# Gate stage of a GNN and mixture-of-experts kernel: one Gelu instead of two, its parts made on VectorE, transposed activations evicted by ScalarE, logits two steps later

## The chip, the cores and the metric

One core of one Trainium2 chip runs the whole program. The metric is the device time of one execution in microseconds. The kernel before was timed three times, and the number given is the median.

## What is computed

The reference, cut to what matters here (the graph layer ahead of it gives `x`, 12500 nodes of 256 features, in float32):

```python
# C = 256, HID = 1024, E = 8, 12500 rows; xf is the layer norm of x
H = gelu(xf @ W1 + b1)                       # 12500 x 1024, exact gelu
probs = softmax(H @ Wg + bg)                 # 12500 x 8
assign = argmax(probs)
out = 0
for e in range(8):
    y = H @ Wd[e] + bd[e]
    out += where(assign == e, probs[:, e] * y, 0)
x = x + out
```

The change touches only the stage that makes `H`, the eight logits of each row and the row's place in the list of its expert.

## The kernel before

The program runs in stages, one after the other: it sorts the edges, sends and collects the messages, runs the two linear layers of the graph part, then the **gate** stage, then the **experts** stage. Each stage is a block in which every engine has its own written-out order of instructions. Semaphores alone tie the engines together; there is no planner.

**The gate stage** (function `gate`, from L1419) walks over 25 chunks of 512 rows (`CN`; chunk number `i`, buffer slot `s` = `i` modulo 2). Each chunk has 8 steps `k` (`KC`), one for each 128 of the 1024 hidden columns. In step `k`:

- TensorE makes `ps_h` (128 hidden columns x 512 rows) from six products of 512 columns (L1857): the inputs are split into a high and a low part in a rounded float format, `w_hi`, `w_lo`, `xnT_hi`, `xnT_lo`. Below this is h(k).
- ScalarE applies Gelu to it twice, once into `act_h` in float32 (L1629) and once into `act_hi`, the rounded high part (L1630). Below, gelu(k).
- VectorE subtracts the two into `act_lo` (L1696, `keep_rest`).
- TensorE turns `act_h` back to rows with four transposes into `ps_b` (L1808, `back`), and adds two products to the logits `ps_g` (L1817 and L1818, `add_logits`). Both are done for step `k - 1` after h(k).
- VectorE copies `ps_b` into the payload `pay` of the chunk (L1705, `keep_back`), for step `k - 1` ahead of `keep_rest(k)`.

`act_h`, `act_hi`, `act_lo`, `ps_h`, `ps_b` and `pay` have two buffers each; `ps_g`, `ps_x`, `gT` and the places have one.

Spread over these steps, at fixed step numbers, is the work of the neighbouring chunks. For the chunk that follows: step 0 turns the graph layer's output (`turn_back` L1790, made ready by ScalarE in `second_output` L1606) and adds the residual (`residual` L1666); step 2 takes the moments of the rows (`moments`, L1671 to L1674 and a chain of small linked instructions); step 4 normalises (L1682); step 5 turns the result (`turn_xn` L1799), and ScalarE (L1612) and VectorE (L1689, `keep_xnT_rest`) split it into high and low. For the chunk that went before: step 0 copies the summed logits (`keep_logits` L1620), step 1 turns them (`turn_logits` L1831) and VectorE chooses the expert (`choose`, L1711 to L1724), step 3 counts (`count`, L1841 and L1844) and finds the places (`find_places`, L1729 to L1740).

When the places of a chunk are known (`where_ready`), GpSimd's queue issues four indirect DMAs (`send`, L1575), which write the chunk's payload of 512 rows x 5168 bytes to the regions of the experts in DRAM, and then copies the next residual into the payload (L1589). A slot of `pay` can be written again only when its four transfers have landed: step 0's eviction of chunk `i` waits for the transfers of chunk `i - 2` (`sent[s]`), which share its slot. That eviction is issued in step 1. With the names of the code, in the chunk's step `k == 1`:

```python
def keep_back(i, s, k, before):
    if k == 0 and later(i, 2):
        dve.wait_ge(sent[s], 16 * CH * before)
```

TensorE's first product to `ps_g` of a chunk (`add_logits(i, 0)`) waits until `keep_logits(i - 1)` has emptied it (`logit_kept`). Instructions that depend on one another on VectorE are tied by `steps.link`, which waits until the first has ended.

Of the kernel before, what the change touches and what calls it, by code (L numbers as in the profile page):

```python
# [11 lines left out]
ACT = mybir.ActivationFunctionType  # L12
AX = mybir.AxisListType

P = 128
# [5 lines left out]
KC = HID // P  # L21
# [3 lines left out]
CH = 4  # L25
# [3 lines left out]
LAST = NCH - 1  # L29
# [45 lines left out]
TTILES = N // P + NE  # L75

RESIDUAL_AT = 0
TURN_LOGITS_AT = 1
CHOOSE_AT = 1
MOMENTS_AT = 2  # L80
COUNT_AT = 3
PLACE_AT = 3
NORMALISE_AT = 4
XN_AT = 5

# [1333 lines left out]
def gate(nc, c, x, w1, b1, wg, bg, wd, hid, expert_w, scale, shift, regions, ends):  # L1419
# [5 lines left out]
    with ExitStack() as ctx:  # L1425
# [8 lines left out]
        act_hi = m.sb("act_hi", [P, 2, CN], F32R)  # L1434
        act_lo = m.sb("act_lo", [P, 2, CN], F32R)
        fold = m.sb("fold", [2 * NE, NE])
        b_sb = m.sb("b_sb", [P, KC])
# [7 lines left out]
        act_h = m.sb("act_h", [P, 2, CN])  # L1445
        pay = m.sb("pay", [P, 2, CH, PAY])
# [25 lines left out]
        ps_h = m.ps("ps_h", [P, 2, CN])  # L1472
        ps_b = m.ps("ps_b", [P, 2, CH, P])
# [37 lines left out]
        def all_chunks(eng, chunk):  # L1511

            chunk(0, 0, 0)
            chunk(1, 1, 0)
            with eng.Fori(1, LAST // 2, 1) as i:
                chunk(2 * i, 0, i)
                chunk(2 * i + 1, 1, i)
            chunk(LAST, 0, LAST // 2)

        def later(i, by=1):  # L1520
            return not isinstance(i, int) or i >= by
# [4 lines left out]
        with nc.Block() as block:  # L1526
# [35 lines left out]
            @block.gpsimd  # L1562
            def _(pool):


                pool.iota(token_i[:], [[P, CH]], base=0, channel_multiplier=1).then_inc(iotas, 1)  # L1566
                pool.iota(first_i[:], [[CAP, PAIRS_E], [CAP - 1, 2]], base=0, channel_multiplier=0).then_inc(iotas, 1)
                pool.iota(sign_i[:], [[0, PAIRS_E], [-2, 2]], base=1, channel_multiplier=0).then_inc(iotas, 1)

                def send(i, s):  # L1570
                    pool.wait_ge(where_ready, i + 1)
                    pool.wait_ge(x2_copied, i + 1)
                    pool.sem_inc(pool_turn, 1)
                    for j in range(CH):
                        pool.indirect_dma_start(  # L1575
                            out=regions[:, :],
                            out_offset=bass.IndirectOffsetOnAxis(ap=where_i[:, s, j:j + 1], axis=0),
                            in_=pay[:, s, j, :], in_offset=None,
                        ).then_inc(sent[s], 16)

                def chunk(i, s, before):
                    if later(i):
                        send(i - 1, 1 - s)

                    if later(i, 2):
                        pool.wait_ge(sent[s], 16 * CH * before)
                    pool.wait_ge(residual_ready, i + 1)
                    pool.sem_inc(pool_turn, 1)
                    pool.tensor_copy(pay[:, s, :, PAY_X:PAY_X + D], x2[:, s]).then_inc(x2_copied, 1)  # L1589

                all_chunks(pool, chunk)
                send(LAST, 0)
                for s in range(2):
                    pool.wait_ge(sent[s], 16 * CH * (LAST // 2 + 1 - s))

            @block.scalar
            def _(act):
                act.wait_ge(params_in, 16 * PARAMS)

                def second_output(i):  # L1600

                    if later(i):
                        act.wait_ge(turned_back, i)
                        act.sem_inc(act_turn, 1)
                    for k in range(DH):
                        ins = act.activation(out2[:, k, :], hid[:, ds(i, 1), k, :].rearrange("p o n -> p (o n)"), ACT.Relu,  # L1606
                                             scale=scale[:, k:k + 1], bias=shift[:, k:k + 1])
                    ins.then_inc(out2_ready, 1)

                def keep_xnT(i, s):  # L1610
                    act.wait_ge(xn_turned, i + 1)
                    act.activation(xnT_hi[:, s], ps_x[:].rearrange("p c f -> p (c f)").rearrange("p (k n) -> p k n", k=DH),  # L1612
                                   ACT.Copy).then_inc(xnT_hi_ready, 1)

                def keep_logits(i):
                    act.wait_ge(logit_sum, i + 1)
                    if later(i):
                        act.wait_ge(logit_done, i)
                        act.sem_inc(act_turn, 1)
                    act.activation(gT[:], ps_g[0:2 * NE, :], ACT.Copy).then_inc(logit_kept, 1)  # L1620

                def chunk(i, s, before):
                    if not is_last(i):
                        second_output(i + 1)
                    for k in range(KC):
                        act.wait_ge(h_done, KC * i + k + 1)

                        act.sem_inc(act_turn, 1)
                        act.activation(act_h[:, k % 2, :], ps_h[:, k % 2, :], ACT.Gelu, bias=b_sb[:, k:k + 1])  # L1629
                        act.activation(act_hi[:, k % 2, :], ps_h[:, k % 2, :], ACT.Gelu, bias=b_sb[:, k:k + 1]).then_inc(h_ready, 1)  # L1630
                        if k == 0 and later(i):
                            keep_logits(i - 1)
                        if k == XN_AT and not is_last(i):
                            keep_xnT(i + 1, 1 - s)

                second_output(0)
                keep_xnT(0, 0)
                all_chunks(act, chunk)
                keep_logits(LAST)

            @block.vector
            def _(dve):
# [49 lines left out]
                def keep_rest(i, k):  # L1692

                    dve.wait_ge(h_ready, KC * i + k + 1)
                    dve.sem_inc(dve_turn, 1)
                    dve.tensor_tensor(act_lo[:, k % 2, :], act_h[:, k % 2, :], act_hi[:, k % 2, :].bitcast(F32),  # L1696
                                      ALU.subtract).then_inc(act_lo_ready, 1)

                def keep_back(i, s, k, before):

                    if k == 0 and later(i, 2):

                        dve.wait_ge(sent[s], 16 * CH * before)
                    dve.wait_ge(back_done, KC * i + k + 1)
                    dve.tensor_copy(pay[:, s, :, k * P:(k + 1) * P], ps_b[:, k % 2, :, :]).then_inc(back_ready, 1)  # L1705

                def choose(i, s):

# [33 lines left out]
                def chunk(i, s, before):  # L1742
                    steps.restart()
                    for k in range(KC):
                        if k > 0:
                            keep_back(i, s, k - 1, before)
                        elif later(i):
                            keep_back(i - 1, 1 - s, KC - 1, None)
                        keep_rest(i, k)
                        if not is_last(i):  # L1750
                            if k == RESIDUAL_AT:
                                residual(i + 1, 1 - s)
                            if k == MOMENTS_AT:
                                moments(i + 1, 1 - s)
                            if k == NORMALISE_AT:
                                normalise(i + 1, 1 - s)
                            if k == XN_AT:
                                keep_xnT_rest(i + 1, 1 - s)
                        if later(i):
                            if k == CHOOSE_AT:  # L1760
                                choose(i - 1, 1 - s)
                            if k == PLACE_AT:
                                find_places(i - 1, 1 - s)
# [5 lines left out]
                keep_xnT_rest(0, 0)  # L1769
                all_chunks(dve, chunk)  # L1770
                steps.restart()
                keep_back(LAST, 0, KC - 1, None)
                choose(LAST, 0)
                find_places(LAST, 0)

# [4 lines left out]
            def _(pe):  # L1780
# [66 lines left out]
                def chunk(i, s, before):  # L1847
                    for k in range(KC):
# [4 lines left out]
                            pe.wait_ge(h_ready, KC * i + k - 1)  # L1853

                        for q in range(DH):
                            for w, a in ((w_hi, xnT_hi), (w_hi, xnT_lo), (w_lo, xnT_hi)):
                                ins = pe.matmul(ps_h[:, k % 2, :], w[:, q, k * P:(k + 1) * P], a[:, s, q, :],  # L1857
                                                start=(q == 0 and w is w_hi and a is xnT_hi),
                                                stop=(q == DH - 1 and w is w_lo))
# [8 lines left out]
                            count(i - 1)  # L1868
                        if k == XN_AT and not is_last(i):
                            turn_xn(i + 1)  # L1870
                        if k > 0:
                            add_logits(i, k - 1)
                        elif later(i):
                            add_logits(i - 1, KC - 1)
                        if k == 0 and not is_last(i):
                            turn_back(i + 1)

# [1 line left out]
                turn_xn(0)  # L1879
                all_chunks(pe, chunk)  # L1880
                back(LAST, KC - 1)
                add_logits(LAST, KC - 1)
                turn_logits(LAST)
                count(LAST)

# [310 lines left out]
```

## Time and profile before

| | us |
|---|---|
| median of 3 runs (lowest, highest) | 3603.17 (3600.44, 3605.65) |
| the profiled execution, its own time | 3586.81 |
| its span, first to last instruction | 3585.0 |
| gate stage, first VectorE instruction to the last | 2459.5 to 3120.6 |
| busy: TensorE, VectorE, ScalarE, GpSimd | 2979.3, 2553.1, 1208.6, 781.5 |

The profile is of one execution. Busy time of TensorE includes the drain of pipelined matmuls, so neighbouring matmuls overlap: a product of 512 columns is shown with 0.39 us and the next one starts 0.23 us after it. In the same way an instruction of ScalarE or VectorE that does not depend on the one ahead of it starts about 0.1 us before that one's shown end. Distances between starts are therefore the safer measure, and the sections below use them.

### The profile page before, as it was taken

Reading aid. Unit: us, or ns where it says so; the run is one execution under the profiler, and the core shown is the slowest. Engines: PE = TensorE matmul, PEld = TensorE weight load, DVE = VectorE, ACT = ScalarE, POOL = GpSimd, SP = SyncE. Lnnn points to the kernel's source line nnn. Section 1 sums busy time; section 2 is a strip of 40 time slices with the busy share of each in tenths; the row PEclk is TensorE's granted clock in tenths of the full one; section 3 lists DMA queues with packets and bytes.
Section 4 is the critical chain, followed back from the end, with each engine's and each line's share of the span. In section 5 each row is a group of like instructions: output and inputs, shape, how many; then the busy total and the mean of one; then the engine's idle time right before and its main releaser. Section 6 shows DMA issues by size and latency. Waiting matters only on the chain. (4 is left out here: it accounts for less than half of the span.)

```text
span 3585.0 us, 67096 instructions
## 1 busy us (share of the span) xinstructions
PE 2979.3 (83%) x20000; PEld 2445.8 (68%) x20001; DVE 2553.1 (71%) x6181; ACT 1208.6 (34%) x2051; POOL 781.5 (22%) x731
## 2 busy tenths in 40 slices
PE   2666667888888886999999999896898889659998
PEld 1233336777777776888888888444676767559998
DVE  5999977777777775777777777335778787676665
ACT  2221103655656653000000000264454545353332
POOL 1211103555555553000000000000122222212222
PEclk9777887999999998999999999998999999879999
DMA  2323105878888887999999999001233334266664
GB/s 75 140 89 105 56 1 195 312 298 308 311 310 308 318 310 278 329 331 329 332 330 330 334 328 332 7 0 32 111 148 135 147 135 160 119 221 210 211 210 146
DMA packets 214716, 751.08 MB, mean 210 GB/s; under 512 B 28411, under 2 KB 64549, under 8 KB 189430
## 3 DMA queue, kind: packets, MB, share of 16 engines
q1 hardware_dynamic: 130694, 446.18, 36.8%
q0 software_dynamic: 83952, 304.02, 21.7%
q8 instruction: 37, 0.61, 0.1%
q14 instruction: 33, 0.27, 0.0%
HBM read 411.44 MB, written 353.16 MB: 213 GB/s over the span
## 5 line engine op out<-in xcount | busy, mean ns | idle before, releaser
L1214 PE MATMUL coll_ps_sum<-coll_rows,coll_hot 128*128 128x256 f32 x3724 | 823.9, 381 | 18.4 <-DVE coll_hot L1155 18.3
L1214 PEld LDWEIGHTS coll_ps_sum<-coll_rows,coll_hot 128*128 128x128 f32 x3724 | 702.3, 191 | 111.1 <-DVE coll_hot L1155 20.3
L1155 DVE TENSOR_SCALAR coll_hot<-coll_nodes,coll_rows 128x128 f32<-128x128 f32 x1862 | 494.7, 342 | 228.0 <-PE coll_ps_sum L1214 165.6
L915 PE MATMUL send_ps_msg<-send_window,send_pick 128*128 128x256 f32 x3584 | 537.7, 299 | 23.6 <-ACT send_msg L948 17.4
L948 ACT ACTIVATE send_msg<-send_ps_msg 128x1024 f32<-128x1024 f32 x448 | 456.4, 1026 | 279.2 <-PE send_ps_msg L915 196.9
L796 POOL DMA_INDIRECT messages<-send_msg,send_to x448 | 469.7, 1048 | 369.6 <-ACT send_msg L948 213.1
L915 PEld LDWEIGHTS send_ps_msg<-send_window,send_pick 128*128 128x128 f32 x3584 | 472.2, 199 | 29.8 <-ACT send_msg L948 19.1
L839 DVE TENSOR_SCALAR send_pick<-send_ps_local,edges_down 128x1024 fp32r<-128x1024 f32 x224 | 287.6, 1284 | 199.7 <-PE send_ps_local L902 143.4
L1247 ACT ACTIVATE nodes_hid<-coll_ps_turned 128x256 f32 (+1 forms) x98 | 37.5, 383 | 811.2 <-PE coll_ps_turned L1059 811.2
L2130 PE MATMUL exp_ps_y<-exp_w_hi,exp_hT_hi 128*128 x840 | 246.5, 293 | 1.0 <-DVE exp_hT_lo L2082 1.0
L2130 PE MATMUL exp_ps_y<-exp_w_hi,exp_hT_lo 128*128 x840 | 238.1, 283 | 0.0
L2130 PE MATMUL exp_ps_y<-exp_w_lo,exp_hT_hi 128*128 x840 | 237.9, 283 | 0.0
L1629 ACT ACTIVATE gate_act_h<-gate_ps_h,gate_b_sb 128x512 f32<-128x512 f32 x200 | 137.3, 686 | 290.1 <-PE gate_ps_h L1857 289.1
L1566 POOL IOTA gate_token_i<- 128x4 int32 x1 | 0.1, 131 | 1044.1 <-POOLq L1292 1044.1
L1575 POOL DMA_INDIRECT regions<-gate_pay,gate_where_i x100 | 109.9, 1099 | 522.0 <-DVEq L1740 499.2
L538 DVE TENSOR_REDUCE sort_place<-sort_banks 128x8 f32<-128x784 f32 x224 | 186.0, 866 | 20.5 <-PE sort_banks L664 18.5
L2026 ACT ACTIVATE exp_hT_hi<-exp_ps_t 128x1024 fp32r<-128x1024 f32 x105 | 107.7, 1026 | 263.7 <-PE exp_ps_t L2119 263.7
L660 PE MATMUL sort_banks<-sort_offset,edges_spread 128*128 128x396 f16 x448 | 121.5, 358 | 68.0 <-DVE sort_place L538 53.3
L1696 DVE TENSOR_TENSOR gate_act_lo<-gate_act_h,gate_act_hi 128x512 fp32r<-128x512 f32 x200 | 139.4, 697 | 51.0 <-ACT gate_act_hi L1630 50.4
L2002 POOL DMA_INDIRECT out_dram<-exp_res,exp_token x105 | 103.2, 983 | 332.5 <-DVE exp_res L2101 330.6
L2082 DVE TENSOR_TENSOR exp_hT_lo<-exp_ps_t,exp_hT_hi 128x1024 fp32r<-128x1024 f32 x105 | 128.6, 1225 | 60.1 <-ACT exp_hT_hi L2026 60.1
L1705 DVE COPY gate_pay<-gate_ps_b 128x512 f32<-128x512 f32 x200 | 138.0, 690 | 45.2 <-PE gate_ps_b L1808 35.0
(300 smaller groups left out, 5177.0 us busy)
## 6 DMA issues: line engine op xcount, KB each, us to landing
coll_rows<-messages SPq DMA_DIRECT2D x98, 1300.0 KB, 7.5
coll_rows<-messages SPq DMA_DIRECT2D x98, 1170.0 KB, 7.4
exp_pay<-regions SPq DMA_DIRECT2D x105, 646.0 KB
send_window<-node_table SPq DMA_DIRECT2D x112, 256.0 KB
node_table<-sort_both SPq DMA_DIRECT2D x25, 1024.0 KB, 4.3
coll_own<-node_table SPq DMA_DIRECT2D x98, 256.0 KB, 4.5
sort_xt<-in_x_dram SPq DMA_DIRECT2D x24, 512.0 KB, 3.8
gate_xt<-in_x_dram SPq DMA_DIRECT2D x24, 384.0 KB
```

The costliest lines, as they stand in the source:

```text
L538: dve.tensor_reduce(place[:, n % BATCH, 2 * a0:2 * a1].rearrange("p (a u) -> p a u", u=2), ranks[:, a0:a1, 0:2 * NB].rearrange("p a (b u) ...
L796: pool.indirect_dma_start(out=runs_out[:, :], out_offset=bass.IndirectOffsetOnAxis(ap=to[:, s, q:q + 1], axis=0), in_=msg[:, s, q, :, :].r ...
L839: dve.tensor_scalar(pick[:, h * (QJ // 2):(h + 1) * (QJ // 2), :], ps_local[:], k.down[:, 0:1], None, ALU.is_equal).then_inc(pick_ready, 1)
L915: ins = pe.matmul(ps_msg[:, q % 2, a, :], pick[:, q * RUN + a, :], window[:, s, part * D:(part + 1) * D], start=(part == 0), stop=(part == 1))
L948: act.activation(msg[:, s, q, :, 0:D], ps_msg[:, q % 2, :, :], ACT.Copy).then_inc(kept, 1)
L1155: ins = dve.tensor_scalar(hot[:, j, :], nodes[:], rows[:, s, j, ROW_ID:ROW_ID + 1], rows[:, s, j, ROW_W:ROW_W + 1], ALU.is_equal, ALU.mult)
L1214: ins = pe.matmul(ps_sum[:, s, 0:D], hot[:, j, :], rows[:, s, j, 0:D], start=(j == 0), stop=(j == CJ - 1))
L1629: act.activation(act_h[:, k % 2, :], ps_h[:, k % 2, :], ACT.Gelu, bias=b_sb[:, k:k + 1])
L1696: dve.tensor_tensor(act_lo[:, k % 2, :], act_h[:, k % 2, :], act_hi[:, k % 2, :].bitcast(F32), ALU.subtract).then_inc(act_lo_ready, 1)
L1705: dve.tensor_copy(pay[:, s, :, k * P:(k + 1) * P], ps_b[:, k % 2, :, :]).then_inc(back_ready, 1)
L2082: dve.tensor_tensor(hT_lo[:, s], ps_t[:, s], hT_hi[:, s].bitcast(F32), ALU.subtract).then_inc(hT_ready, 1)
L2130: ins = pe.matmul(ps_y[:, s, 0:D], h[:, s, k, :], w[:, ds(e, 1), k, :].rearrange("p o f -> p (o f)"), start=(k == 0 and h is hT_hi and w i ...
```

## The change

ScalarE runs one Gelu for each step, into `act_h`. VectorE makes `act_hi` from it with a copy into the rounded format, and then `act_lo`, linked. The eviction `keep_back` moves from VectorE to ScalarE, behind the Gelu of the step, with its wait for the transfers. The products for the logits of step `k - 2` (`LAG`) are issued between the two halves of h(k). The fixed steps move: `turn_logits` and `choose` from 1 to 2, `count` from 3 to 4, `find_places` from 3 to 5, `keep_logits` from 0 to 1. `send` waits for the last eviction of its chunk as well.

```diff
-TURN_LOGITS_AT = 1
-CHOOSE_AT = 1
+LAG = 2
+TURN_LOGITS_AT = 2
+CHOOSE_AT = 2
 MOMENTS_AT = 2
-COUNT_AT = 3
-PLACE_AT = 3
+COUNT_AT = 4
+PLACE_AT = 5
 NORMALISE_AT = 4
 XN_AT = 5
...
                     pool.wait_ge(x2_copied, i + 1)
+                    pool.wait_ge(back_ready, KC * (i + 1))
...
+                def keep_back(i, s, k, before):
+                    if k == 0 and later(i, 2):
+                        act.wait_ge(sent[s], 16 * CH * before)
+                    act.wait_ge(back_done, KC * i + k + 1)
+                    act.sem_inc(act_turn, 1)
+                    act.activation(pay[:, s, :, k * P:(k + 1) * P], ps_b[:, k % 2, :, :], ACT.Copy).then_inc(back_ready, 1)
...
                         act.sem_inc(act_turn, 1)
-                        act.activation(act_h[:, k % 2, :], ps_h[:, k % 2, :], ACT.Gelu, bias=b_sb[:, k:k + 1])
-                        act.activation(act_hi[:, k % 2, :], ps_h[:, k % 2, :], ACT.Gelu, bias=b_sb[:, k:k + 1]).then_inc(h_ready, 1)
-                        if k == 0 and later(i):
+                        act.activation(act_h[:, k % 2, :], ps_h[:, k % 2, :], ACT.Gelu, bias=b_sb[:, k:k + 1]).then_inc(h_ready, 1)
+                        if k > 0:
+                            keep_back(i, s, k - 1, before)
+                        elif later(i):
+                            keep_back(i - 1, 1 - s, KC - 1, None)
+                        if k == LAG - 1 and later(i):
                             keep_logits(i - 1)
...
                     dve.sem_inc(dve_turn, 1)
+                    steps.link(dve.tensor_copy(act_hi[:, k % 2, :], act_h[:, k % 2, :]))
                     dve.tensor_tensor(act_lo[:, k % 2, :], act_h[:, k % 2, :], act_hi[:, k % 2, :].bitcast(F32),
                                       ALU.subtract).then_inc(act_lo_ready, 1)
-                def keep_back(i, s, k, before):
-                    if k == 0 and later(i, 2):
-                        dve.wait_ge(sent[s], 16 * CH * before)
-                    dve.wait_ge(back_done, KC * i + k + 1)
-                    dve.tensor_copy(pay[:, s, :, k * P:(k + 1) * P], ps_b[:, k % 2, :, :]).then_inc(back_ready, 1)
...
                     for k in range(KC):
-                        if k > 0:
-                            keep_back(i, s, k - 1, before)
-                        elif later(i):
-                            keep_back(i - 1, 1 - s, KC - 1, None)
                         keep_rest(i, k)
...
                         for q in range(DH):
+                            if q > 0 and k >= LAG:
+                                add_logits(i, k - LAG)
+                            elif q > 0 and later(i):
+                                add_logits(i - 1, KC + k - LAG)
                             for w, a in ((w_hi, xnT_hi), (w_hi, xnT_lo), (w_lo, xnT_hi)):
...
-                        if k > 0:
-                            add_logits(i, k - 1)
-                        elif later(i):
-                            add_logits(i - 1, KC - 1)
```

After the last chunk the two products of both last steps follow one another, and ScalarE's last eviction stands ahead of the last `keep_logits`.

## Rows read from the trace of the kernel before

**Rows 1.** Busy time by engine, two chunks: stretch, length, busy (count), clock, DMA.

```profile
2700.00:2751.20 51.20, 45.13 (x270) 35.49 (x268) 40.36 (x113) 25.73 (x41) 11.03 (x11) 0.97 0.39 144
```

**Rows 2.** Who waited for whom, 2600 to 2900 us: total, times, longest.

```profile
PE gate_ps_g L1817 <- DVE gate_act_lo L1696: 27.0, 11, 2.5
```

**Rows 3.** TensorE in order of time: start, us, operation, idle before it.

```profile
2697.76 0.39 PE L1817 MATMUL gate_ps_g<-gate_act_hi,gate_wg_parts 128*16 128x512 f32 x1 [2.46 <-DVE gate_act_lo L1696]
...
2701.34 1.09 PE L1799 MATMUL gate_ps_x<-all_ident,gate_turns 128*128 128x128 f32 x8 [1.15 <-DVE gate_turns L1682]
...
2704.49 0.47 PE L1817 MATMUL gate_ps_g<-gate_act_hi,gate_wg_parts 128*16 128x512 f32 x1
...
2706.41 0.60 PE L1808 MATMUL gate_ps_b<-all_ident,gate_act_h 128*128 128x128 f32 x4
2706.76 0.47 PE L1817 MATMUL gate_ps_g<-gate_act_hi,gate_wg_parts 128*16 128x512 f32 x1
...
2709.61 1.03 PE L1790 MATMUL gate_ps_x<-all_ident,gate_turns 128*128 128x128 f32 x8
2710.40 0.48 PE L1857 MATMUL gate_ps_h<-gate_xnT_hi,gate_w_hi 128*128 128x512 f32 x1
...
2749.00 0.39 PE L1817 MATMUL gate_ps_g<-gate_act_hi,gate_wg_parts 128*16 128x512 f32 x1 [2.46 <-DVE gate_act_lo L1696]
```

**Rows 4.** VectorE in order of time, one chunk and the next one's start.

```profile
2699.91 1.38 DVE L1682 TENSOR_SCALAR gate_turns<-gate_x,gate_mv,gate_rstd 128x256 f32<-128x256 f32 x4
...
2703.64 1.23 DVE L1689 TENSOR_TENSOR gate_xnT_lo<-gate_ps_x,gate_xnT_hi 128x1024 fp32r<-128x1024 f32 x1 [1.15 <-issue]
...
2708.11 0.69 DVE L1696 TENSOR_TENSOR gate_act_lo<-gate_act_h,gate_act_hi 128x512 fp32r<-128x512 f32 x1 [0.37 <-ACT gate_act_hi L1630]
...
2714.19 0.18 DVE L1711 TENSOR_TENSOR gate_logit<-gate_ps_p,gate_bg_sb 128x32 f32<-128x32 f32 x1
...
2715.95 0.69 DVE L1705 COPY gate_pay<-gate_ps_b 128x512 f32<-128x512 f32 x1
...
2717.56 1.40 DVE L1671 BATCH_NORM_STATS2 gate_stats<-gate_x 128x6 f32<-128x256 f32 x4
...
2721.79 0.69 DVE L1705 COPY gate_pay<-gate_ps_b 128x512 f32<-128x512 f32 x1
...
2722.99 0.18 DVE L1729 TENSOR_TENSOR gate_place<-gate_ps_p,gate_first 128x32 f32<-128x32 f32 x1
...
2725.38 1.38 DVE L1682 TENSOR_SCALAR gate_turns<-gate_x,gate_mv,gate_rstd 128x256 f32<-128x256 f32 x4
...
2738.52 0.69 DVE L1705 COPY gate_pay<-gate_ps_b 128x512 f32<-128x512 f32 x1 [0.30 <-PE gate_ps_b L1808]
```

**Rows 5.** ScalarE in order of time, from one step to the next chunk's first.

```profile
2706.70 0.69 ACT L1629 ACTIVATE gate_act_h<-gate_ps_h,gate_b_sb 128x512 f32<-128x512 f32 x1 [1.00 <-PE gate_ps_h L1857]
2707.28 0.68 ACT L1630 ACTIVATE gate_act_hi<-gate_ps_h,gate_b_sb 128x512 fp32r<-128x512 f32 x1
2707.85 1.51 ACT L1606 ACTIVATE gate_turns<-nodes_hid,all_shift,all_scale 128x512 f32 x2
...
2710.41 0.57 ACT L1620 ACTIVATE gate_gT<-gate_ps_g 16x512 f32<-16x512 f32 x1
```

**Rows 6.** VectorE's copies from SBUF into the rounded format, at the stage's start.

```profile
2459.47 1.23 DVE L1647 CAST gate_w_hi<-gate_pay 128x2048 fp32r<-128x2048 f32 x1 [8.69 <-DMA gate_b_sb<-in_L_ffn_b_dram]
2460.73 0.19 DVE L1648 CAST gate_wg_parts<-gate_wg_sb 128x64 fp32r<-128x64 f32 x1
```

**Rows 7.** GpSimd's queue in order of time: the sends of one chunk.

```profile
2724.93 1.39 POOL L1575 DMA_INDIRECT regions<-gate_pay,gate_where_i  x1 [19.22 <-DVEq L1740]
2726.62 0.97 POOL L1575 DMA_INDIRECT regions<-gate_pay,gate_where_i  x1 [0.30 <-issue]
```

**Rows 8.** Busy time by engine around the end of these transfers; last three: clock, DMA share, GB/s.

```profile
2733.50:2734.00 0.50, 0.50 (x4) 0.41 (x3) 0.17 (x1) 0.50 (x2) 0.00 (x0) 1.00 0.33 124
```

**Rows 9.** The same view where TensorE's clock falls.

```profile
2720.50:2723.90 3.40, 0.94 (x6) 0.53 (x5) 3.02 (x14) 1.22 (x2) 0.00 (x0) 1.00 0.00 0
2723.90:2727.30 3.40, 3.40 (x13) 2.64 (x12) 2.92 (x8) 0.97 (x2) 2.07 (x2) 0.51 0.13 55
```

More of the change, by code:

```diff
@@ L1638, in _ @@
                 all_chunks(act, chunk)
+                keep_back(LAST, 0, KC - 1, None)
                 keep_logits(LAST)
@@ L1771, in _ @@
                 steps.restart()
-                keep_back(LAST, 0, KC - 1, None)
                 choose(LAST, 0)
@@ L1881, in _ @@
                 back(LAST, KC - 1)
-                add_logits(LAST, KC - 1)
+                for k in range(KC - LAG, KC):
+                    add_logits(LAST, k)
                 turn_logits(LAST)
```

## The prediction, as put on record before the changed kernel was run

> **What bounds the kernel now.** The change touches the gate stage alone, so I read that stage. First the busy time by engine over two chunks [rows 1]: TensorE is busy 45.1 of 51.2 us, VectorE 40.4, ScalarE 25.7. The stage is near TensorE's bound but idles 3.0 us per chunk. Then the waits [rows 2]: TensorE loses 2.5 us in each chunk to `act_lo`. Then the engines in order of time. The waiting product for the logits starts at 2697.76 and, two chunks later, at 2749.00 [rows 3]: a chunk takes 25.62 us. VectorE's order explains the wait: `moments` holds it from 2717.56 to 2721.79, 4.23 us [rows 4], and `keep_back` and `keep_rest` of the next step stand behind it. A second idle, 1.15 us, is `turn_xn` waiting for `normalise` [rows 3], the next thing in the same chain of VectorE. So the chunk is set by a loop through both engines: gelu(2), `moments`, `keep_rest` of steps 3 and 4, `normalise`, `turn_xn`, and then TensorE's steps 6, 7, 0, 1, 2.
>
> The last thing to see is the payload. The places start at 2722.99, the first send at 2724.93 [rows 4, 7], and in the half microsecond from 2733.50 the DMA share is 0.33 where it was near 1, so the last transfer ends near 2733.66 [rows 8]. The eviction that waits for these transfers starts at 2738.52 [rows 4]. The cover is 4.9 us today.
>
> **The change, part by part.** A plain step of TensorE takes 2706.76 - 2704.49 = 2.27 us, of which 0.35 are the four transposes (2706.41 to 2706.76) and 1.92 eight products, 0.24 each [rows 3]. Neither the number of products nor of transposes changes, so TensorE has the same work.
>
> ScalarE gives up a Gelu (0.58 from start to start, rows 5) and takes on a copy of the same size from PSUM. `keep_logits` is a copy of 512 elements per partition and lasts 0.57 [rows 5]; with the overlap that the Gelus show I take 0.50, at most 0.58. ScalarE's total stays as it is.
>
> VectorE gives up eight copies of 0.60 a chunk (2721.79 to 2722.99 holds two instructions, rows 4) and takes on eight copies from SBUF to the rounded format. The trace has none of 512 elements, but it has 64 in 0.19 and 2048 in 1.23 us [rows 6]; the line between them gives 0.43. Bounds: 0.31, a quarter of the large one, and 0.69, the copy out of PSUM [rows 4]. I take 0.43, so `keep_rest` costs 0.43 + 0.60 = 1.03, against 1.20 for the pair before. VectorE's busy time falls from 20.2 to 18.1 us a chunk.
>
> The wait for `act_lo` in step 4 goes: the products now come a step and a half later. But the fixed steps move too. `choose` (2714.19 to 2715.95, 1.76 us, rows 4) now stands right behind `moments` in step 2, and `find_places` stands behind `keep_xnT_rest` in step 5. Follow one chunk from the start of gelu(2), called 0:
>
> - gelu ends at 0.69, hand-over 0.15 (2707.28 + 0.68 to 2708.11, rows 5 and 4): `keep_rest(2)` runs 0.84 to 1.87.
> - `moments` 4.23, to 6.10; `choose` 1.76, to 7.86; `keep_rest` of steps 3 and 4, to 9.92. TensorE waits for `chosen` at `count` meanwhile, then follows.
> - `normalise` start to `turn_xn` start is 1.43 (2699.91 to 2701.34, rows 4 and 3): `turn_xn` at 11.35. From there to `keep_xnT_rest` 2.30 (to 2703.64), and 1.14 for itself (1.23 less the overlap of 0.09, rows 4): 14.79.
> - `find_places` to the first send 1.94 (2722.99 to 2724.93): send at 16.73. First send to landed 8.73 (to 2733.66): 25.46.
>
> When is the slot wanted? TensorE: `turn_xn` 11.35 + 0.79 (as `turn_back`, 2709.61 to 2710.40, rows 3) = 12.14; h(6) + 1.92 = 14.06; h(7) 16.33; h(0) of the next chunk 18.60; transposes 18.95. `turn_back` waits for `second_output`: gelu(7) starts 0.29 after its products (2706.41 to 2706.70), at 16.62, then 0.58, 0.50, 1.51 and 0.15 [rows 5], so 19.36; + 0.79 + 1.92 puts h(1) at 22.07, gelu(1) at 22.36, and `keep_back(0)` could run at 22.94. It must wait until 25.61, 2.67 us more. Today's cover is gone and the wait sits on ScalarE's queue.
>
> What is queued behind it: `keep_logits` (0.57) and gelu(2). TensorE waits for `keep_logits`, because `add_logits(0)` stands in the middle of h(2). So: `keep_back` 25.61 + 0.50, `keep_logits` + 0.57 = 26.68, hand-over 0.15, two products 0.48 and three 0.72: h(2) at 28.03, and the next gelu(2) starts at 28.32. The new loop is 28.32 long: it runs from the places through the transfers to the logits and back.
>
> That is 2.70 us over 25.62. It is paid in every chunk from number 2 to 24, 23 times: +62 us. To it I add 0.35 us a chunk, 8 us in all. First, the link behind the copy and the transfers' signal are not free. Second, the clock: today TensorE idles most of 2720.5 to 2723.9 and the next 3.4 us are granted 0.51, the lower of its levels, 1.2 GHz [rows 9], and the new idle, some 3.5 us ahead of the logits, is longer. The 1.2 us of products behind it would take 2.4 at that level, if it fell there each time. I take part of that. Sum: +70 us, so 3586.8 + 70 = 3657 for an execution like the profiled one, 3603.2 + 70 = 3673 against the median, which lies 16 us above the profiled one.
>
> If the copies collide with the sends: the first send above lasts 1.39 against 0.97 for the second [rows 7], and `normalise` runs in that time (from 2725.38, rows 4). The Trainium skill, page "SBUF — State Buffer", section "Who interferes with whom", has it that a VectorE copy or cast in its two-port mode and a GpSimd instruction shut each other out entirely while they run. By that rule a new copy could hold up the first send for its 0.43 us; 23 x 0.43 would make the sum +80 instead of +70. The later sends have room: with 0.97 each and 0.30 between, the fourth is issued 5.2 us after the first has begun, and the last transfer ends at 8.73.
>
> **The rivals.** *The payload lands in time* (no new wait). If the places came 2.67 us earlier in the chunk, or the transfers were 2.67 us quicker, the loop would be VectorE's again: 28.32 - 2.67 = 25.65 us, as today, for the time that `choose` adds behind `moments` eats what the lighter `keep_rest` and the single Gelu give. Time 3603; with the copy at 0.69 (three in the loop, 0.78 us a chunk) 3621. For it: today's cover of 4.9 us is not small, and all hand-overs are read from one chunk. Against it: the wait comes out with a margin of more than half of the gaps that I estimated.
>
> *TensorE becomes the bound* (the other side, faster). The wait for `act_lo`, 2.5 us a chunk, goes, nothing takes its place, and the chunk shrinks to TensorE's own 22.6 us (45.13 / 2, rows 1): 24 chunks x 3.02 are 73 us less, 3530. For it: VectorE's busy time falls to 18.1, ScalarE's stays at 13, so by shares there is room. It decides if `normalise` ends before TensorE has h(5), and the sends land before `keep_back(0)`. Against it: the chain of VectorE from gelu(2) to `turn_xn` is 11.35 long, while TensorE needs for h(3), h(4) and h(5) three plain steps, 6.8 us, and the short `turn_logits` and `count`.
>
> *The copy runs at 0.69*, and the transfers bind too: + 0.78 x 23 = 18 more, 3691.
>
> **How the numbers follow.** The sends bind: 0.86, of which the copy at 0.69 holds 0.10 and a partly hidden wait (a loop of 26.5 to 28 us, +20 to +55) 0.14. Its own range: copy at 0.31 and nothing for clock and signals, 62 - 8 = +54, 3657; copy at 0.69 and the clock low behind each wait, 62 + 18 + 27 = +107, 3710. In time, as today: 0.07. TensorE bound, or part of that gain: 0.07. The range reaches down to the partly hidden wait: 3630 to 3710. A measurement of this kernel can tell about 0.2%, 7 us, from no change: faster 0.07, same 0.05 (the in-time case with the quick copy), slower 0.88.
>
> **What the profile of the changed kernel would show.** Chunks of 28 to 29 us between like instructions. The new eviction on ScalarE for step 0 starts when the DMA share has just fallen to nothing, with an idle of 2 to 3.5 us before it, and the same step's Gelu and `keep_logits` right behind. TensorE idle 3 us or more ahead of the first product for the logits in the middle of h(2), and some 2 us at `count`. The casts at 0.43. No idle ahead of L1817 caused by `act_lo`. Wrong would be: first sends that start less than 16 us after gelu(2), transfers that end in under 8 us, or an idle of ScalarE at that eviction which ends with TensorE's transposes.

## The result and the profile after

The changed kernel is slower: 3720.18 us (median of 4, 3718.68 to 3724.81) against 3604.41 us before (median of 4), a ratio of 1.0326 with a 95% interval of 1.031 to 1.0343. That is +116 us; +70 was forecast, and the range ended at 3710. The sign and the mechanism were right; the size was too small.

The profiled execution took 3718.68 us. Nearly all of the difference lies in the gate stage. From the start of its first VectorE instruction to the start of its last it took 661.0 us before (2459.47 to 3120.45) and takes 781.8 us now (2468.81 to 3250.63): +120.8. It also starts 9.3 us later, behind stages that the change doesn't touch: the profiled execution of before, 3586.81 us, was 18 us under its median. A chunk takes 30.7 us from send to send in the middle of the stage, against 25.6.

Who waited for whom in the changed kernel, 2600 to 3000 us (total, times, longest):

```profile
PE gate_ps_g L1821 <- ACT gate_gT L1632: 52.9, 13, 4.1
ACT gate_pay L1625 <- DMA regions<-gate_pay,gate_where_i: 41.3, 13, 3.3
```

TensorE's wait for `act_lo` [rows 2] is gone from the list. In its place ScalarE's eviction (L1625) waits 3.2 us in each chunk for the transfers of the sends, and TensorE waits 4.1 us for `keep_logits` (L1632), which stands behind that eviction.

ScalarE in order of time, from one gelu(2) to the next (start, us, operation, idle before it):

```profile
2702.70 0.69 ACT L1641 ACTIVATE gate_act_h<-gate_ps_h,gate_b_sb 128x512 f32<-128x512 f32 x1 [2.57 <-PE gate_ps_h L1865]
...
2725.90 0.69 ACT L1641 ACTIVATE gate_act_h<-gate_ps_h,gate_b_sb 128x512 f32<-128x512 f32 x1 [2.06 <-PE gate_ps_h L1865]
2729.73 0.60 ACT L1625 ACTIVATE gate_pay<-gate_ps_b 128x512 f32<-128x512 f32 x1 [3.13 <-DMA regions<-gate_pay,gate_where_i]
2730.22 0.57 ACT L1632 ACTIVATE gate_gT<-gate_ps_g 16x512 f32<-16x512 f32 x1
2733.35 0.69 ACT L1641 ACTIVATE gate_act_h<-gate_ps_h,gate_b_sb 128x512 f32<-128x512 f32 x1 [2.56 <-PE gate_ps_h L1865]
```

The loop of the forecast is all here: eviction, logits copy, and 2.6 us later the Gelu of step 2. VectorE in the same chunk (answers to rows 4 and 6):

```profile
2703.53 0.43 DVE L1712 CAST gate_act_hi<-gate_act_h 128x512 fp32r<-128x512 f32 x1 [4.80 <-ACT gate_act_h L1641]
...
2704.60 1.40 DVE L1687 BATCH_NORM_STATS2 gate_stats<-gate_x 128x6 f32<-128x256 f32 x4
...
2708.83 0.19 DVE L1720 TENSOR_TENSOR gate_logit<-gate_ps_p,gate_bg_sb 128x32 f32<-128x32 f32 x1
...
2710.76 0.43 DVE L1712 CAST gate_act_hi<-gate_act_h 128x512 fp32r<-128x512 f32 x1 [0.24 <-DVE gate_token L1733]
...
2712.33 0.43 DVE L1712 CAST gate_act_hi<-gate_act_h 128x512 fp32r<-128x512 f32 x1 [0.41 <-ACT gate_act_h L1641]
...
2713.40 1.38 DVE L1698 TENSOR_SCALAR gate_turns<-gate_x,gate_mv,gate_rstd 128x256 f32<-128x256 f32 x4
...
2717.14 1.23 DVE L1705 TENSOR_TENSOR gate_xnT_lo<-gate_ps_x,gate_xnT_hi 128x1024 fp32r<-128x1024 f32 x1 [0.92 <-ACT gate_xnT_hi L1615]
2718.28 0.18 DVE L1738 TENSOR_TENSOR gate_place<-gate_ps_p,gate_first 128x32 f32<-128x32 f32 x1
```

TensorE at `turn_xn` and then around its long wait, and GpSimd's first sends (answers to rows 3 and 7):

```profile
2714.83 1.09 PE L1803 MATMUL gate_ps_x<-all_ident,gate_turns 128*128 128x128 f32 x8 [0.29 <-DVE gate_turns L1698]
...
2730.93 0.58 PE L1821 MATMUL gate_ps_g<-gate_act_hi,gate_wg_parts 128*16 128x512 f32 x1 [4.03 <-ACT gate_gT L1632]
2731.32 0.63 PE L1822 MATMUL gate_ps_g<-gate_act_lo,gate_wg_parts 128*16 128x512 f32 x1
2731.74 0.63 PE L1865 MATMUL gate_ps_h<-gate_xnT_hi,gate_w_hi 128*128 128x512 f32 x1
...
2732.60 0.63 PE L1865 MATMUL gate_ps_h<-gate_xnT_hi,gate_w_lo 128*128 128x512 f32 x1
2733.02 1.05 PE L1812 MATMUL gate_ps_b<-all_ident,gate_act_h 128*128 128x128 f32 x4
```

```profile
2720.26 1.39 POOL L1578 DMA_INDIRECT regions<-gate_pay,gate_where_i  x1 [24.38 <-DVEq L1749]
2721.96 1.07 POOL L1578 DMA_INDIRECT regions<-gate_pay,gate_where_i  x1 [0.30 <-issue]
```

Behind the wait the products start 0.43 us apart instead of 0.23: TensorE runs at the lower of its two levels, 1.2 GHz (the granted clock from 2730 to 2734 is 0.50). Busy time by engine (the last three columns are granted clock, DMA share, GB/s) around the end of the transfers, and over this chunk:

```profile
2728.50:2729.00 0.50, 0.00 (x0) 0.00 (x0) 0.47 (x2) 0.00 (x0) 0.00 (x0) 1.00 0.93 372
2729.00:2729.25 0.25, 0.00 (x0) 0.00 (x0) 0.25 (x1) 0.00 (x0) 0.00 (x0) 1.00 0.54 37
```

```profile
2702.70:2733.35 30.65, 26.30 (x136) 19.47 (x135) 18.67 (x56) 12.41 (x20) 5.43 (x5) 0.83 0.32 119
```

The granted clock is 0.83 over the chunk; it was 0.97 [rows 1]. The large transfers end at about 2729.0, and the eviction that waits for them starts at 2729.73.

### The profile page after: what moved, and what is told of

Its sections match the earlier page's. It is cut to its first block and busy times, and to the rows that moved or that the text cites. A ratio compares the mean times of both kernels' runs of the same rounds, so it can differ in the third digit from the quotient of the medians.

```text
span 3716.9 us, 67295 instructions
## 1 busy us (share of the span) xinstructions
PE 3068.4 (83%) x20000; PEld 2485.9 (67%) x20001; DVE 2515.0 (68%) x6181; ACT 1195.5 (32%) x2051; POOL 780.6 (21%) x731
## 5 line engine op out<-in xcount | busy, mean ns | idle before, releaser
L1216 PE MATMUL coll_ps_sum<-coll_rows,coll_hot 128*128 128x256 f32 x3724 | 823.6, 380 | 18.9 <-DVE coll_hot L1157 18.8
L1216 PEld LDWEIGHTS coll_ps_sum<-coll_rows,coll_hot 128*128 128x128 f32 x3724 | 700.4, 190 | 113.4 <-DVE coll_hot L1157 20.8
L1712 DVE CAST gate_act_hi<-gate_act_h 128x512 fp32r<-128x512 f32 x200 | 86.3, 432 | 203.7 <-ACT gate_act_h L1641 182.8
L1865 PE MATMUL gate_ps_h<-gate_xnT_hi,gate_w_hi 128*128 128x512 f32 x400 | 193.1, 483 | 2.5 <-DVE gate_xnT_lo L1705 2.5
L1865 PE MATMUL gate_ps_h<-gate_xnT_lo,gate_w_hi 128*128 128x512 f32 x400 | 174.5, 436 | 0.0
L1865 PE MATMUL gate_ps_h<-gate_xnT_hi,gate_w_lo 128*128 128x512 f32 x400 | 174.4, 436 | 0.0
```

The costliest lines, as they stand in the source:

```text
L1216: ins = pe.matmul(ps_sum[:, s, 0:D], hot[:, j, :], rows[:, s, j, 0:D], start=(j == 0), stop=(j == CJ - 1))
```

## The experiments

Nine variants and one repetition ran on three other chips: `logits_copy_first`, `places_step4`, `filler_products` and `before_steps_moved` on one, `places_ahead_of_xnT` and `early_moments_lag1` on another, the rest on the third. There the kernel before takes 3468 to 3470 us. The stages ahead of the gate stage are shorter: it starts at 2340.9 us in the changed kernel, not at 2468.8. The gate stage itself is the same: 781.8 us for the changed kernel on the first chip and 781.9 on the other. So each kernel is set against the kernel before on its own chip, and where two variants are compared, it is by these differences. "Chunk" is the distance from one GpSimd payload copy to the next in the middle of the stage.

| kernel | against before, us | ratio (95% interval) | gate stage, us | chunk, us |
|---|---|---|---|---|
| changed (`after_again`) | +122.5 | 1.0347 (1.0331, 1.0363) | 781.9 | 30.7 |
| filler_products | +100.9 | 1.0291 (1.0274, 1.0308) | 757.9 | 29.7 |
| before_steps_moved | +44.4 | 1.0122 (1.0105, 1.0139) | 706.4 | 27.3 |
| places_ahead_of_xnT | +42.7 | 1.0123 (1.0106, 1.0139) | 703.3 | 27.4 |
| logits_copy_first | +40.4 | 1.0115 (1.0098, 1.0132) | 700.4 | 27.3 |
| places_step4 | +23.3 | 1.0064 (1.0047, 1.008) | 681.8 | 26.4 |
| split_alone | +5.4 | 1.0008 (0.9999, 1.0017) | 666.0 | 25.8 |
| early_moments_old_split | -15.1 | 0.9951 (0.9936, 0.9966) | 647.1 | 24.9 |
| early_moments_lag1 | -19.2 | 0.9945 (0.9929, 0.9962) | 645.1 | 24.8 |
| early_moments | -51.1 | 0.9843 (0.9828, 0.9858) | 608.7 | 23.2 |

**The changed kernel again** (`after_again`).

> The changed kernel as it is, on the same chip as the runs beside it, so that they can be subtracted from it. Theory A says nothing new of it: a chunk of 30.7 us and 116 us over the kernel before. If its gate stage differed from the one of the first profile by more than 5 us, the gate stages of different chips couldn't be compared.

Measured: 3590.67 us, +122.5, chunk 30.7, gate stage equal within 0.1 us. The gate stage can be compared across these chips.

**Who stands behind the wait** (`logits_copy_first`).

```diff
-                        if k > 0:
-                            keep_back(i, s, k - 1, before)
-                        elif later(i):
-                            keep_back(i - 1, 1 - s, KC - 1, None)
                         if k == LAG - 1 and later(i):
                             keep_logits(i - 1)
+                        if k > 0:
+                            keep_back(i, s, k - 1, before)
+                        elif later(i):
+                            keep_back(i - 1, 1 - s, KC - 1, None)
```

> The changed kernel with one edit: in step 1 ScalarE runs keep_logits ahead of the eviction of step 0 that waits for the sends. Theory A (the loop runs places, sends, eviction, keep_logits, logits product, h(2), gelu(2)): the copy of the logits and the products behind it, 0.5 + 0.15 + 2.1 + 0.3 us, leave the loop, and gelu(2) starts right behind the eviction. A chunk falls from 30.65 to between 26.8 and 27.6 us; 23 chunks make 3630 to 3650 us. TensorE's idle ahead of the first logits product falls from 4 us to under 1, and ScalarE still waits for the sends. Rival B (the time is TensorE's lower clock, set off by its idles of any kind): the idle only moves to another product, and the time stays near 3700.

Measured: +40.4 us against before, 82 less than the changed kernel; chunk 27.3. ScalarE in order of time:

```profile
2715.64 0.57 ACT L1632 ACTIVATE gate_gT<-gate_ps_g 16x512 f32<-16x512 f32 x1
2719.01 0.60 ACT L1625 ACTIVATE gate_pay<-gate_ps_b 128x512 f32<-128x512 f32 x1 [2.80 <-DMA regions<-gate_pay,gate_where_i]
2719.51 0.68 ACT L1641 ACTIVATE gate_act_h<-gate_ps_h,gate_b_sb 128x512 f32<-128x512 f32 x1
```

The wait for the sends is still there, 2.8 us, but the Gelu of step 2 follows the eviction at once. So the loop through the logits copy is real, and 82 us hang on the order of two instructions. TensorE still idles, now at `count` (2600 to 2900 us: total, times, longest):

```profile
PE gate_ps_p L1848 <- DVE gate_chosen L1732: 36.7, 11, 3.4
```

Rival B expected the time to stay when the idle only moves. It didn't, and B falls.

**When the places are found** (`places_step4`, `places_ahead_of_xnT`).

```diff
-PLACE_AT = 5
+PLACE_AT = 4
```

> The changed kernel with one number changed: find_places in step 4 (behind normalise) instead of step 5 (behind keep_xnT_rest). Theory A: the first send starts 3.5 us earlier in the chunk, the eviction's wait of 3.1 us goes, and the loop is VectorE's again, about 25.8 us without the lower clock, up to 26.5 with it: 3600 to 3625 us, no difference from the kernel before. Rival C (the eviction on ScalarE and the copy on VectorE themselves cost the time, by contention with the sends): the chunk stays near 30 us and the time near 3715.

```diff
                             if k == XN_AT:
+                                if later(i):
+                                    find_places(i - 1, 1 - s)
                                 keep_xnT_rest(i + 1, 1 - s)
...
-                            if k == PLACE_AT:
+                            if k == PLACE_AT and is_last(i):
                                 find_places(i - 1, 1 - s)
```

> The changed kernel with find_places still in step 5, but ahead of keep_xnT_rest instead of behind it. It fills an idle of VectorE and adds no work; the first send starts 2.1 us earlier in the chunk. Theory A: while the sends bind, every microsecond of an earlier send is a microsecond of the chunk: 30.7 falls to 28.6 us, 48 us under the changed kernel (3543 us on this chip), and the wait of ScalarE for the sends stays. A lower clock that also lets go would make it 60. Rival E (the wait for the sends is hidden behind something else): no change.

Measured: with step 4 the wait for the sends is gone, the chunk is 26.4 us and 99 of 122 us are back. No difference from the kernel before was expected, 3625 us at most; 3604.4 + 23.3 is 3 us above that. With the places ahead of `keep_xnT_rest`, the chunk falls by 3.4 us to 27.4, and the time by 80 us where 48, or 60 with the clock, were expected. The first send of that kernel, its waiting eviction and the next gelu(2):

```profile
2710.09 0.98 POOL L1578 DMA_INDIRECT regions<-gate_pay,gate_where_i  x1 [21.57 <-DVEq L1749]
```

```profile
2719.24 0.60 ACT L1625 ACTIVATE gate_pay<-gate_ps_b 128x512 f32<-128x512 f32 x1 [0.87 <-DMA regions<-gate_pay,gate_where_i]
...
2721.90 0.69 ACT L1641 ACTIVATE gate_act_h<-gate_ps_h,gate_b_sb 128x512 f32<-128x512 f32 x1 [1.59 <-PE gate_ps_h L1867]
```

and its busy time by engine over 300 us:

```profile
2600.00:2900.00 300.00, 259.46 (x1474) 190.36 (x1474) 211.16 (x615) 135.64 (x220) 56.52 (x55) 0.95 0.37 137
```

The sends still bind, by 0.9 us there, and the clock has risen from 0.83 to 0.95. The gelu(2) ahead of these rows starts at 2694.42, so the first send comes 15.67 us after it, 1.9 earlier than in the changed kernel. From first send to eviction it takes 9.15 us instead of 9.47, and from eviction to gelu(2) 2.66 instead of 3.62, which is the clock. These three parts make 3.2 us in this chunk, of 3.4 in the mean. Rivals C and E fall: no work was moved between engines in either kernel.

**What the lower clock costs** (`filler_products`). Twelve more products of 512 columns, whose result is not used:

```diff
                         for q in range(DH):
+                            if q > 0 and k == LAG and later(i, 2):
+                                pe.wait_ge(back_ready, KC * i)
+                                for _ in range(FILL):
+                                    pe.matmul(ps_b[:, 1, :, :].rearrange("p c f -> p (c f)"), w_hi[:, 0, 0:P], xnT_hi[:, s, 0, :],
+                                              start=True, stop=True)
```

> The changed kernel with 12 more products of 512 columns in the middle of h(2), ahead of the wait for the logits buffer, into a buffer that is overwritten afterwards; the result is not used. They fill 2.8 of the 4.0 us that TensorE idles there. It measures the share of the lower clock. If the clock is worth what the walk leaves over (0.9 us in the products behind the wait and 0.8 us in the later start of normalise), a chunk falls from 30.65 to about 29 us although TensorE does more: 3680 us, and the granted clock is 1.00 in the chunk. If the clock is worth nothing, 3720 us. If the products start at the lower clock they last 5.1 us and the chunk grows by 1 us: 3745 us.

Measured: 21.6 us less than the changed kernel (100.9 against 122.5), although TensorE does 2.8 us more in each chunk; 40 were expected. Its stage in the view by engine, and ScalarE around the wait:

```profile
2600.00:2900.00 300.00, 265.71 (x1473) 198.79 (x1474) 188.02 (x570) 124.03 (x201) 54.27 (x50) 0.96 0.33 123
```

```profile
2715.15 0.60 ACT L1626 ACTIVATE gate_pay<-gate_ps_b 128x512 f32<-128x512 f32 x1 [3.19 <-DMA regions<-gate_pay,gate_where_i]
2715.64 0.57 ACT L1633 ACTIVATE gate_gT<-gate_ps_g 16x512 f32<-16x512 f32 x1
2717.80 0.69 ACT L1642 ACTIVATE gate_act_h<-gate_ps_h,gate_b_sb 128x512 f32<-128x512 f32 x1 [1.58 <-PE gate_ps_h L1871]
```

The wait for the sends is as long as in the changed kernel. From the eviction to gelu(2) it takes 2.65 us where the changed kernel takes 3.62. That 0.97 us is the price of the lower clock behind the wait, and 0.97 x 23 = 22 us accounts for the whole difference.

The smaller part, in steps 3 and 4, came back and was lost again. In the chunk whose gelu(2) starts at 2688.06:

```profile
2695.86 0.18 PE L1849 MATMUL gate_ps_p<-gate_chosen,all_after 128*128 128x8 bf16 x1 [1.71 <-DVE gate_chosen L1733]
...
2700.28 1.04 PE L1804 MATMUL gate_ps_x<-all_ident,gate_turns 128*128 128x128 f32 x8
```

```profile
2698.25 1.38 DVE L1699 TENSOR_SCALAR gate_turns<-gate_x,gate_mv,gate_rstd 128x256 f32<-128x256 f32 x4
```

```profile
2698.00:2699.00 1.00, 1.00 (x4) 0.79 (x3) 1.00 (x4) 0.00 (x0) 0.00 (x0) 0.50 0.00 0
```

With gelu(4) in time, `normalise` starts 10.19 us after gelu(2), 0.51 sooner than in the changed kernel. But TensorE, now ahead of VectorE, idles 1.7 us at `count`, the clock falls to 0.50 behind that, and `turn_xn` starts at 12.22, where it was 12.13. `places_step4` shows the same: `normalise` at 10.2, `turn_xn` at 11.6 to 12.3. The forecast, at the full clock, had 11.35.

**The step numbers or the split** (`before_steps_moved`, `split_alone`). The first is the kernel before with `TURN_LOGITS_AT = 2`, `CHOOSE_AT = 2`, `COUNT_AT = 4`, `PLACE_AT = 5`; the second is the changed kernel with `LAG = 1`, `add_logits` at its old place and every step number of before.

> The kernel before with the step numbers of the changed one alone: turn_logits and choose in step 2, count in 4, find_places in 5; both Gelus, the eviction on VectorE and the old place of the logits products stay. Theory A: the sends are as late as in the changed kernel, and VectorE waits for them at its eviction: a chunk of 27.2 us by the same walk, more with the lower clock, so 35 to 70 us over the kernel before, 3640 to 3675 us. Rival C (the cause is the work moved between the engines, not the step numbers): no more than 5 us over the kernel before.

> The kernel before with the split alone: one Gelu, act_hi by VectorE, evictions by ScalarE, and send's new wait; the logits products stay one step behind and every step number is that of the kernel before. Theory A: the sends leave at step 3 as before and the wait for them does not bind; VectorE's chain gets three times 0.17 us shorter and the single Gelu 0.58, but the copy stands in the chain of act_lo: a chunk of about 25.3 us, 10 us under the kernel before. Rival C (the moved work costs by itself): 20 us or more over the kernel before.

Measured: the step numbers alone cost 44 us, as expected, and VectorE waits for the sends in that kernel (2600 to 2900 us):

```profile
DVE gate_pay L1705 <- DMA regions<-gate_pay,gate_where_i: 16.3, 11, 1.6
```

The split alone costs 5 us with an interval that touches no change; a gain of 10 was expected. So a third of the loss is the steps by themselves, and the split by itself is next to nothing. The other 73 us come only when everything is together. Both kernels here have the logits one step behind; the lag of two, which brings `keep_logits` behind the waiting eviction in step 1, was not tried alone. `logits_copy_first` shows the link: only with the waiting eviction on ScalarE, ahead of `keep_logits` and gelu(2), does the late send hold up TensorE's logits.

**A version that beats both** (`early_moments`, with two that take it apart).

```diff
-MOMENTS_AT = 2
+MOMENTS_AT = 1
-PLACE_AT = 5
+PLACE_AT = 4
-NORMALISE_AT = 4
+NORMALISE_AT = 3
```

and the order of `logits_copy_first`.

> The changed kernel with keep_logits ahead of the waiting eviction and three numbers: moments in step 1, normalise in step 3, find_places in step 4. Theory A: VectorE's long block lies a step earlier than choose, TensorE no longer waits at count or turn_xn, the sends leave 3.5 us earlier, and the chunk comes near TensorE's own 22.6 to 23.5 us: 50 to 70 us under the kernel before. Rival D (the lower clock stays, whatever the idles): a chunk above 25 us.

> The kernel before (two Gelus, eviction by VectorE, logits one step behind) with the same steps as early_moments: turn_logits and choose in 2, count and find_places in 4, moments in 1, normalise in 3. Theory A: VectorE has 20.2 us of work in a chunk against 18.1, and act_lo has one step less of slack: about 24 us a chunk, 30 to 45 us under the kernel before, between it and early_moments. If it came out as quick as early_moments, the split and the lag would be worth nothing in themselves.

> The split of the changed kernel (one Gelu, VectorE's two parts, ScalarE's eviction) and the steps of early_moments, but the logits products one step behind and at their old place. It parts the lag from the split. If the slack of the later logits carries the gain, it lies near early_moments_old_split, 24.5 us a chunk or more, 15 to 25 us under the kernel before. If the lighter VectorE carries it, it comes within 10 us of early_moments, 23.2 to 23.6 us a chunk.

Measured: -51 us, a chunk of 23.2 us, both within what was expected, towards its weak end. Busy time by engine over 300 us, and what is left of the idle at the logits buffer:

```profile
2600.00:2900.00 300.00, 289.38 (x1731) 214.54 (x1731) 241.71 (x728) 156.71 (x259) 72.65 (x65) 1.00 0.42 155
```

```profile
2719.44 0.39 PE L1821 MATMUL gate_ps_g<-gate_act_hi,gate_wg_parts 128*16 128x512 f32 x1 [0.30 <-ACT gate_gT L1632]
```

TensorE is busy 96% of the time at the full clock, so this is close to its bound, and rival D falls. With the same steps and the old split 15 us are gained (30 to 45 expected), with the new split and the old lag 19, the case expected if the later logits carry the gain. The split alone is worth 4 us there; the logits two steps later, with `keep_logits` ahead of the eviction, are worth 32. In both kernels with the old lag TensorE waits for `act_lo` again.

## Why the prediction was right or wrong

**What bounds the stage, and the new loop: right.** The loop of places, sends, eviction, `keep_logits`, logits product and gelu(2) is what runs. This table sets the forecast walk beside the changed kernel's chunk from 2702.70; times are from the start of gelu(2).

| | forecast | measured |
|---|---|---|
| first cast of `keep_rest(2)` | 0.84 | 0.83 |
| `moments` | 1.87 | 1.90 |
| `choose` | 6.10 | 6.13 |
| `keep_rest(3)` | 7.86 | 8.06 |
| `keep_rest(4)` | 8.89 | 9.63 |
| `normalise` | 9.92 | 10.70 |
| `turn_xn` | 11.35 | 12.13 |
| `keep_xnT_rest` | 13.65 | 14.44 |
| `find_places` | 14.79 | 15.58 |
| first send | 16.73 | 17.56 |
| waiting eviction | 25.61 | 27.03 |
| first logits product | 26.83 | 28.23 |
| h(2) done | 28.03 | 30.32 |
| next gelu(2) | 28.32 | 30.65 |

**The copy: right.** 0.43 us, interpolated from 64 and 2048 elements. Two of the signs named are absent. The chunks last 30.7 us and not 28 to 29. And TensorE doesn't idle 2 us at `count`, since at the lower clock h(3) and h(4) come so late that `choose` is done. One side figure was misread: VectorE's busy time was to fall to 18.1 us a chunk and is 18.67. The sum took off the shown durations, which overlap; by the distances between starts, 8 x 0.17 off 20.2, it gives 18.8.

**The step that failed is the allowance for clock and signals**, 0.35 us a chunk, 8 us in all. The table shows 2.33 us a chunk over the walk, 54 us in 23 chunks, and 62 + 54 = 116, of the 120.8 that the stage lost. It has three parts:

- TensorE's lower clock behind the wait: five products take 2.09 us (2730.93 to 2733.02) and not 1.20. +0.89. The forecast named this as 1.2 us if the clock fell there each time, and took "a part of that". It falls each time. `filler_products` shows 0.97.
- The clock again in steps 3 and 4: gelu(4) comes late, and `keep_rest(4)` waits for it (0.41 us idle in the row at 2712.33). Together with the links behind the copies and a gap of 0.24 behind `choose` this makes +0.78 at `normalise`, of which some 0.5 is the late Gelu: in `filler_products`, with gelu(4) in time, `normalise` starts 0.51 us sooner.
- The signal of the transfers: the first send to the end of the large transfers is 2729.0 - 2720.26 = 8.7 us, as forecast, but the eviction starts 0.7 us after that end where 0.15 was taken. +0.59 over both. The end is read off the fall of the DMA rate, so how the 0.59 parts between transfer and signal is rough.

The error was to treat the clock as a share to be guessed. The rows of before showed one fall in two chunks behind an idle of 2.5 us; the new idle was forecast at 3.5 us, in every chunk, right ahead of products inside the binding loop. That calls for the full price, which was in the upper bound: 62 + 27 for the clock gives 3692, still 28 us short. Even the upper end of 3710 held no signal time and only one place for the clock.

**The rival "in time"** didn't occur in the changed kernel, but `places_step4` is its condition made true: 26.4 us a chunk where the walk without the wait gave 25.65. Its `turn_xn` starts 0.3 to 0.95 us behind the walk; in the chunk from 2684.35 it is 0.76 us late, and the clock is 0.50 from 2693 to 2696 ahead of it. **The rival "TensorE bound"** needed `normalise` early and the sends landed. `early_moments` grants both, and the chunk is 23.2 us where 22.6 was its price. **The port pair**: from the Trainium skill's rule (page "SBUF — State Buffer", section "Who interferes with whom") the prediction worked out 10 us for a held-up first send. The first send lasts 1.39 us after as before, the second 1.07 against 0.97, and from first send to the end of the transfers nothing changed. No part of the loss is seen there. Nor was `normalise` what made the first send longer than the second: it has ended at 2714.8, well ahead of the send at 2720.26. In `places_ahead_of_xnT` the first send lasts 0.98; what sets it is not shown.

## What to carry to other kernels

When a wait moves to another engine, list what stands behind it there: the late sends cost 44 us with the eviction in VectorE's queue. The full change, with it in ScalarE's queue ahead of the copy that frees the logits buffer, cost 122, and swapping those two instructions gave 82 us back. When a step number moves later, follow its result round to the next use of the same buffer. And where the traces show the clock falling behind an idle of TensorE, as here behind waits of 1.7 to 4.0 us, an idle inside the loop that binds is paid twice, once as the wait and once at the lower clock behind it; take both in full.

## What the runs showed of the hardware

A small shift of a wait moved the time by more than itself. First sends 1.9 us earlier made the chunk 3.4 us shorter, with the granted clock up from 0.83 to 0.95; 1.0 of it is the stretch behind the wait, back at the full clock. And the changed kernel's chunks in the middle of the stage all lasted 30.7 us on both chips while those of `places_step4` varied between 25.8 and 26.9.

VectorE's cast collided with GpSimd, in `early_moments` and once a chunk:

```profile
2715.26 1.06 POOL L1592 COPY gate_pay<-gate_x 128x1024 f32<-128x1024 f32 x1
```

```profile
2715.74 0.86 DVE L1712 CAST gate_act_hi<-gate_act_h 128x512 fp32r<-128x512 f32 x1 [1.31 <-ACT gate_act_h L1641]
```

The cast lasts 0.43 otherwise (0.68 once, beside a send). Here it ends 0.28 us after GpSimd's copy ends at 2716.32. Without their fixed part, 512 elements take 0.27 us by the line through [rows 6], so it is as if the cast had begun to move data only then. In one chunk it starts later, 0.30 us ahead of the copy's end, lasts 0.59, and again ends 0.29 us after it. That agrees with the Trainium skill, page "SBUF — State Buffer", section "Who interferes with whom", by which the one that comes second is shut out until the first is done. What it cost is not measured; TensorE is busy 96% of the time all the same.
